# Cross attention and quantised FFN on one core: transposes of the activations moved from TensorE to DMA, with row-group bias matmuls, a deeper pipeline and another prologue

## The chip, the cores and the metric

The kernel runs on one core of one Trainium2 chip. The metric is device time in microseconds (us), the median of several executions; lower is better. The core has TensorE (PE in the rows; PEld is its weight load), VectorE (DVE), ScalarE (ACT), GpSimd (POOL), and SyncE (SP), which here only issues DMAs.

## The reference

x has 4 x 2048 rows of 512, the context 4 x 154 rows of 512. First cross attention with a mask `j % 2048 == i`: since the context has only 154 rows, query i < 154 sees only key i, and a query i >= 154 sees none, so its softmax is uniform over all 154. Queries and keys drop out: row i of the attention is `V[i] @ Wout + bout`, or the mean of V put through Wout. Then a feed-forward layer on 8-bit activations and ternary weights:

```
x = x + attention(context)
h = layernorm(layernorm(x)) * gamma + beta
xq, sx = round(h * 127 / max|h|), 127 / max|h|      # per row
h = gelu((xq @ w1q.T) / (sx * sw1) + b1)            # 512 -> 2048
hq, sh = round(h * 127 / max|h|), 127 / max|h|
x = x + (hq @ w2q.T) / (sh * sw2) + b2              # 2048 -> 512
```

w1q and w2q are `clip(round(w / mean|w|), -1, 1)`, made on the chip; sw1 and sw2 are the weight scales, `1 / mean|w|`.

## The kernel before, in words

The 8192 rows are 64 tiles of 128 rows (rotated by two tiles, so that the first need only the mean row of batch 0). Every engine has a program of its own, written out by hand in order; semaphores tie them. The main part is a loop of steps s = 0..66 in which each engine works on tiles at different distances.

Weights are in SBUF as bf16 (`w1q`, `w2q`). A matmul contracts over the 128 partitions, so both activations must be brought into the form [feature, row] first. TensorE does that with an identity matrix:
- `transpose_h` (L684 to L689) turns the rounded x tile, 4 blocks of 128x128, into PSUM `p_xT` (L688); ACT copies it out to `xqT` (`evac_x`, L416).
- L738 does the same with the rounded hidden tile `hround`, 16 blocks into `p_hT`; ACT copies them out in two halves to `hqT` (L452).

In step s TensorE does: the hidden transposes of tile s-2, layer one of tile s (L751, 16 matmuls into the four banks of `p_ffn1`), the x transposes of tile s+1, layer two of tile s-2 (L766, 16 matmuls into `p_y`). DVE adds the bias to layer one with the scale `xdeq` and takes it out of PSUM (L572, two halves), ACT applies the gelu in place (L438), DVE takes the maximum (L579) and makes the step and the scale (L582, L585), ACT rounds (L459). DVE then adds layer two's result to x (L654), SP stores it (L261). DVE's statistics and maximum (L544, L534) and POOL's additions of attention, gamma, beta and b2 (L290, L302, L304, L322), its rounding (L311) and small scale operations (L308, L315) feed the x side.

The prologue multiplies Wv and Wout first (`wvo`, L695, fp32), then the context rows with the product (L708 tail rows, L713 the four times 128 first rows), and makes the ternary weights (L500 to L504, L411). The mean row is spread over a tile by L718.

Of the kernel before, what the change touches and what calls it, by code (L numbers as in the profile page):

```python
# [6 lines left out]
I16 = mybir.dt.int16  # L40
ALU = mybir.AluOpType
# [3 lines left out]
P = 128  # L45
# [17 lines left out]
MAGIC = ROUND + OFFSET


def block_program(nc, x, ctxT, wvT, wout, bout, w1T, b1, w2T, b2, gamma, beta, out, tail_rows):
    es = ExitStack()
    with es:
# [6 lines left out]
        def sem(name):  # L75
# [33 lines left out]
        xdeq = sb("xdeq", [P, 8])  # L109
        hmax = sb("hmax", [P, 8])  # L110
# [22 lines left out]
        ones = sb("ones", [P, P])  # L133


        p_ffn1 = ps("p_ffn1", [P, HID])
        p_hT = ps("p_hT", [P, KH, P], BF16)
        p_xT = ps("p_xT", [P, KD, 2 * P], BF16)
        p_y = ps("p_y", [P, D])
        p_mean = p_xT[:, :, :].rearrange("p k n -> p (k n)").bitcast(FP32)  # L140
        p_wsum = p_hT[:, :, :].rearrange("p k n -> p (k n)").bitcast(FP32)


        ins_loaded = [sem(f"ins_loaded{i}") for i in range(KI)]
        ctx_loaded = sem("ctx_loaded")
        w1_loaded = [sem(f"w1_loaded{k}") for k in range(2)]
        w2_loaded = [sem(f"w2_loaded{k}") for k in range(4)]
        vec_loaded = sem("vec_loaded")
        b1_loaded = sem("b1_loaded")
        ones_set, ident_set = sem("ones_set"), sem("ident_set")  # L150
        wvo_done, wvo_copied = sem("wvo_done"), sem("wvo_copied")
        ctx_means, tail_gathered = sem("ctx_means"), sem("tail_gathered")
        attn_done, attn_copied = sem("attn_done"), sem("attn_copied")
        mean_done, mean_copied = sem("mean_done"), sem("mean_copied")
        pick_set = sem("pick_set")
        tail_stored = sem("tail_stored")
        attn_spread = [sem(f"attn_spread{b}") for b in range(B)]
        wparts_done = [sem(f"wparts_done{j}") for j in range(2)]
# [8 lines left out]
        x_loaded = [sem(f"x_loaded{r}") for r in range(8)]  # L167
# [3 lines left out]
        xstd_done, xgamma_done, xnormed = sem("xstd_done"), sem("xgamma_done"), sem("xnormed")  # L171
        xmax_done, xstep_done, xscale_ready = sem("xmax_done"), sem("xstep_done"), sem("xscale_ready")
        xdeq_ready, xround_done = sem("xdeq_ready"), sem("xround_done")
        xT_done, xqT_ready = sem("xT_done"), sem("xqT_ready")
        ffn1_done, bias_done, gelu_done = sem("ffn1_done"), sem("bias_done"), sem("gelu_done")
        hmax_done, hstep_done, hscale_ready = sem("hmax_done"), sem("hstep_done"), sem("hscale_ready")
        hdeq_ready, hround_done = sem("hdeq_ready"), sem("hround_done")
        hT_done, hqT_ready = sem("hT_done"), sem("hqT_ready")
        ffn2_done, y_ready = sem("ffn2_done"), sem("y_ready")
        y_stored = [sem(f"y_stored{r}") for r in range(4)]  # L180

        def col(t, c):

            return t[:, c % 8:c % 8 + 1]

        def live(i, c, ahead):

            return not isinstance(i, int) or 0 <= BODY * i + c + ahead < T

        def run(eng, step, first=0):  # L190


            for s in range(first, T + 3):
                step(s // BODY, s % BODY)

        def w_piece(j, n):

            return w1_raw[n // 2][:, n % 2, :] if j == 0 else w2_raw[:, n * HID:(n + 1) * HID]

        def wq_piece(j, n):  # L200

            return w1q[:, n, :] if j == 0 else w2q[:, 4 * n:4 * n + 4, :].rearrange("p k n -> p (k n)")

        block = es.enter_context(nc.Block())


        @block.sync
# [594 lines left out]
```

## Time and profile before

| | |
|---|---|
| median of 3 runs | 596.89 us (596.06 to 596.98) |
| profiled execution | 597.54 us |
| its span | 595.7 us |
| matmuls of layer one, tile 0, start | 61.31 us |
| matmuls of layer one, tile 3 | 87.93 to 91.33 us |
| one tile in the middle of the run | 8.03 us |
| granted TensorE clock, mean | 0.986 |

The span is from the first to the last instruction in the profile. A group's mean is the duration of one instruction; matmuls overlap, so the distance between two is shorter than the duration of one. "Idle before" is the time that the engine stood still ahead of the group, with what ended it behind the arrow.

### The profile page before, as it was taken

What the parts mean: (1) busy time and instruction counts of PE and PEld (TensorE: products, weight loads), DVE (VectorE), ACT (ScalarE), POOL (GpSimd) and SP (SyncE); (2) the same over time, 40 slices, a digit from 0 to 9 for tenths busy, and PEclk for the clock granted to TensorE, in tenths of its full rate; (3) what the DMA queues carried; (4) which work ended last, traced back from release to release, by engine and by line L of the source; (5) the groups of instructions that cost most, each with busy time, mean ns of one, the idle gap of its engine ahead of it and who ended that gap; (6) DMA issues with size and microseconds to landing.
All of it is one profiled execution on the core that took longest, in us unless ns stands there. A gap on an engine that the chain in (4) does not pass through costs nothing.

```text
span 595.7 us, 9691 instructions
## 1 busy us (share of the span) xinstructions
PE 568.9 (95%) x3374; PEld 295.4 (50%) x3438; DVE 513.4 (86%) x803; ACT 434.6 (73%) x412; POOL 449.9 (76%) x584
## 2 busy tenths in 40 slices
PE   6979777999999999999999999999999999999996
PEld 2434333555555555555555555555555555555553
DVE  0286998999999999999999999999999999998773
ACT  0046854787887788788778878877877787787784
POOL 0006879999898888889888988988888898887410
PEclk9979888999999999999999999999999999999999
DMA  8986512222221222222122222222222221300011
GB/s 317 411 278 244 173 30 60 72 72 71 72 53 57 71 73 70 72 72 54 55 70 73 72 70 72 48 62 71 70 73 72 72 49 58 89 36 19 37 36 54
DMA packets 26438, 53.24 MB, mean 89 GB/s; under 512 B 2729, under 2 KB 2729, under 8 KB 25749
## 3 DMA queue, kind: packets, MB, share of 16 engines
q1 hardware_dynamic: 24708, 49.25, 26.8%
q10 hardware_dynamic: 1680, 3.36, 1.6%
q8 instruction: 28, 0.46, 0.3%
q14 instruction: 22, 0.17, 0.1%
HBM read 35.60 MB, written 17.00 MB: 88 GB/s over the span
## 4 chain that ended last, share of the span: by engine, by line
PE 84%; DVE 7%; DMA 4%; issue 2%; POOL 1%; ACT 1%; ACTq 1%; POOLq 0%
PE p_y L766 36%; PE p_ffn L751 34%; PE p_hT L738 9%; DMA xb<-ctxT 4%; PE p_xT L688 2%; DVE hid L572 1%; DVE hmax L579 1%; PE p_y L708 1%; DVE wpart L509 1%; ACTq L400 1%; POOL x L290 1%; DVE hx L528 1%; DVE stat L544 1%; DVE w2q L504 1%; DVE xb L477 0%
## 5 line engine op out<-in xcount | busy, mean ns | idle before, releaser
L766 PE MATMUL p_y<-w2q,hqT 128*128 128x512 bf16 x1023 | 234.8, 383 | 7.0 <-DVE y L654 3.5
L751 PE MATMUL p_ffn<-w1q,xqT 128*128 128x512 bf16 x961 | 219.6, 381 | 6.9 <-ACT xqT L416 3.7
L459 ACT ACTIVATE hround<-hid,hscale 128x2048 f32<-128x2048 f32 x64 | 128.2, 2003 | 74.6 <-DVE hscale L585 74.6
L572 DVE SCALAR_TENSOR_TENSOR hid<-p_ffn,xdeq,b_b 128x1024 f32<-128x1024 f32 x128 | 163.4, 1279 | 0.6 <-issue 0.6
L766 PEld LDWEIGHTS p_y<-w2q,hqT 128*128 128x128 bf16 x1024 | 98.3, 99 | 116.1 <-issue 5.4
L751 PEld LDWEIGHTS p_ffn<-w1q,xqT 128*128 128x128 bf16 x1024 | 97.8, 98 | 111.3 <-ACT xqT L416 3.7
L579 DVE TENSOR_REDUCE hmax<-hid 128x1 f32<-128x2048 f32 x64 | 145.6, 2275 | 0.1
L438 ACT ACTIVATE hid<-hid 128x1024 f32<-128x1024 f32 x128 | 134.4, 1051 | 14.9 <-DVE hid L572 14.9
L452 ACT ACTIVATE hqT<-p_hT 128x1024 bf16<-128x1024 int16 x128 | 123.9, 1020 | 23.4 <-PE p_hT L738 23.4
L290 POOL TENSOR_TENSOR x<-x,attn 128x512 f32<-128x512 f32 x64 | 81.7, 1278 | 46.6 <-ACT attn L422 46.6
L304 POOL TENSOR_TENSOR hx<-hx,beta_b 128x512 f32<-128x512 f32 x63 | 80.6, 1279 | 4.9
L302 POOL TENSOR_TENSOR hx<-hx,gamma_b 128x512 f32<-128x512 f32 x63 | 81.0, 1286 | 1.8 <-DVE hx L528 1.8
L322 POOL TENSOR_TENSOR xb<-x,b_b 128x512 f32<-128x512 f32 x64 | 81.8, 1278 | 0.0
L654 DVE SCALAR_TENSOR_TENSOR y<-p_y,hdeq,xb 128x512 f32<-128x512 f32 x64 | 48.0, 750 | 37.3 <-PE p_y L766 37.2
L738 PEld LDWEIGHTS p_hT<-ident,hround 128*128 128x128 bf16 x1024 | 62.4, 98 | 16.4 <-ACT hround L459 2.0
L308 POOL TENSOR_TENSOR xdeq<-xstep,wmean 128x1 f32<-128x1 f32 x64 | 28.5, 446 | 53.6 <-DVE xscale L676 49.3
L738 PE MATMUL p_hT<-ident,hround 128*128 128x128 bf16 x1024 | 67.6, 219 | 1.1 <-ACT hround L459 1.1
L311 POOL TENSOR_SCALAR hx<-hx,xscale 128x512 f32<-128x512 f32 x64 | 44.9, 701 | 0.0
L544 DVE BATCH_NORM_STATS2 stat<-x 128x6 f32<-128x512 f32 x64 | 43.7, 683 | 1.2 <-POOL x L290 1.2
L534 DVE TENSOR_REDUCE xmax<-hx 128x1 f32<-128x512 f32 x64 | 43.3, 676 | 1.7 <-POOL hx L304 1.7
L296 POOL TENSOR_TENSOR rstd<-var_e,neg_half 128x1 f32<-128x1 f32 x64 | 35.8, 559 | 5.3
L416 ACT ACTIVATE xqT<-p_xT 128x512 bf16<-128x512 int16 x64 | 36.9, 576 | 0.8 <-PE p_xT L688 0.8
(58 smaller groups left out, 286.7 us busy)
## 6 DMA issues: line engine op xcount, KB each, us to landing
x<-x SPq DMA_DIRECT2D x64, 256.0 KB, 3.0
out<-y SPq DMA_DIRECT2D x64, 256.0 KB, 3.2
raw<-w2T SPq DMA_DIRECT2D x4, 1024.0 KB, 9.1
raw<-wout ACTq DMA_DIRECT2D x8, 256.0 KB, 7.7
raw<-wvT SPq DMA_DIRECT2D x8, 256.0 KB, 7.1
hid<-w1T SPq DMA_DIRECT2D x2, 1024.0 KB, 14.9
hround<-w1T SPq DMA_DIRECT2D x2, 1024.0 KB, 20.2
attn<-tail_rows SPq DMA_DIRECT2D x7, 256.0 KB
```

Of the source, the lines that this page charges most:

```text
L290: pool.tensor_tensor(x1[:, c, :], x1[:, c, :], a, ALU.add).then_inc(x1_ready, 1)
L302: pool.tensor_tensor(h, h, gamma_b[:, :], ALU.mult).then_inc(xgamma_done, 1)
L304: pool.tensor_tensor(h, h, beta_b[:, :], ALU.add).then_inc(xnormed, 1)
L322: pool.tensor_tensor(xb[:, c % 8, :], x1[:, c % 8, :], b2_b[:, :], ALU.add)\
L438: nc.scalar.activation(g, g, ACT.Gelu).then_inc(gelu_done, 1)
L452: nc.scalar.activation(hqT[:, c % 2, 8 * h:8 * h + 8, :], p_hT[:, 8 * h:8 * h + 8, :].bitcast(I16), ACT.Copy, bias=-float(OFFSET)).then_in ...
L459: nc.scalar.activation(hround[:, (c - 1) % 2, :], hid[:, (c - 1) % 2, :], ACT.Copy, scale=col(hscale, c - 1), bias=MAGIC).then_inc(hround_ ...
L572: nc.vector.scalar_tensor_tensor(hid[:, c % 2, h * HALF:(h + 1) * HALF], p_ffn1[:, h * HALF:(h + 1) * HALF], col(xdeq, c), b1_b[:, h * HAL ...
L579: nc.vector.tensor_reduce(col(hmax, c), hid[:, c % 2, :], AX.X, ALU.max, apply_absolute_value=True).then_inc(hmax_done, 1)
L738: tr = nc.tensor.transpose(p_hT[:, k, :], low[:, k * P:(k + 1) * P], ident[:, :])
L751: mm = nc.tensor.matmul(p_ffn1[:, n * D:(n + 1) * D], xqT[:, c % 2, k, :], w1q[:, k, n * D:(n + 1) * D], start=(k == 0), stop=(k == KD - 1))
L766: mm = nc.tensor.matmul(p_y[:, :], hqT[:, c % 2, k, :], w2q[:, k, :], start=(k == 0), stop=(k == KH - 1))
```

## The change

- **x transposed by DMA.** ACT rounds x to 16-bit integers (`xi`), POOL widens them to bf16 (`xq`), SP issues a transposing DMA of 128 x 640 elements of 2 bytes (`transpose_x`, L213) into `xqT`. The fifth block of 128 columns holds 1 / (scales) of the row, split in three bf16 parts.
- **Hidden tile transposed by DMA.** ACT rounds to 8-bit integers (`hq8`, L486); SP issues a transposing DMA over them as 16-bit words, two features to a word (`transpose_h`, L221), into `hT8`; DVE and ACT each widen one half to bf16 in `hqT` (L656, L493). The rows of `w2q` are laid out in pairs to fit.
- **Bias by matmul.** The four matmuls of L801 take the fifth block, 32 partitions for each bank, times `b1rows` (b1 in three bf16 parts), with `tile_position=(32 * g, 0)`; so the accumulated PSUM times `xdeq` contains b1, and ACT's gelu reads PSUM itself (L479). DVE's L572 is gone.
- **Layer two three tiles behind** (`LAG = 3`, was 2), `p_y` in two banks (`py`), x tiles in a ring of 16 in which the result is made in place.
- **x side:** gamma is applied by DVE together with the mean (L623), the factor 1/std by ACT (L464), statistics and scales for two tiles at a time, POOL's additions over two tiles at once.
- **Prologue:** V^T = Wv^T ctx^T is made first (L770 for the tail, L784 for the main rows), then times Wout (L749, and L760 in the first three steps of the main loop); weights are loaded in other pieces on both queues; b1 is split by POOL and stored by 12 small DMAs.

```diff
-                if live(i, c, -2):
-                    pe.wait_ge(hround_done, s - 1)
...
-                    for k in range(KH):
-                        tr = nc.tensor.transpose(p_hT[:, k, :], low[:, k * P:(k + 1) * P], ident[:, :])
...
-                if live(i, c, 1):
-                    pe.wait_ge(xqT_ready, s + 1)
-                    transpose_h(s + 1, c + 1)
...
+            for s in range(T + LAG):
+                if live(s):
+                    pe.wait_ge(xT_landed[s % 4], 16 * (s // 4 + 1))
...
+                        pe.wait_ge(gelu_done, 2 * s)
+                    xT = xqT[:, (s // 2) % 2, s % 2, :, :]
+                    for g in range(4):
+                        nc.tensor.matmul(p1[:, g * D:(g + 1) * D], xT[32 * g:32 * g + 32, KD, :],
+                                         b1rows[32 * g:32 * g + 32, :], start=True, stop=False,
+                                         tile_position=(32 * g, 0))
...
+                if s == 0:
+                    out_rows(1, pa[:, :])
+                elif s == 1:
+                    weight_total(1)
+                    out_rows(2, py[:, 0, :])
+                elif s == 2:
+                    out_rows(3, py[:, 1, :])
+                    pe.wait_ge(wmean_done[1], 1)
+                    out_rows(0, pb[:, :])
...
+                    pe.wait_ge(hcast_dve, t + 1)
+                    pe.wait_ge(hcast_act, t + 1)
```

```diff
+            def transpose_h(t):
+                sp.wait_ge(hround_done, t + 1)
+                if t >= 2:
+                    sp.wait_ge(hcast_dve, t - 1)
+                    sp.wait_ge(hcast_act, t - 1)
+                sp.dma_start_transpose(hT8[:, t % 2, :].bitcast(I16).rearrange("p (j n) -> p j n", j=NJ),
+                                       hq8[:, t % 2, :].bitcast(I16)).then_inc(hT_landed[t % 4], 16)
...
+            for s in range(T + LAG + 2):
+                if live(s - LAG - 1):
+                    t = s - LAG - 1
+                    sp.wait_ge(y_ready, t + 1)
+                    sp.dma_start(out[t * P:(t + 1) * P, :], xr[:, t % XS, :]).then_inc(y_stored[t % XS], 16)
+                if live(s - 1):
+                    transpose_h(s - 1)
...
+                if s >= 3 and live(s + 11):
+                    load_x(s + 11)
...
+                if s % 2 == 1:
+                    for t in (s + 3, s + 4):
+                        if live(t):
+                            transpose_x(t)
```

ACT and DVE in the main loop of the changed kernel:

```diff
+                if live(s - 1):
+                    round_h(s - 1)
+                if live(s):
+                    gelu(s, 0)
+                if live(s - 2):
+                    widen_h(s - 2)
+                if live(s):
+                    gelu(s, 1)
+                if s % 2 == 0:
+                    for t in (s + 4, s + 5):
+                        if live(t):
+                            times_std(t)
+                else:
+                    for t in (s + 3, s + 4):
+                        if live(t):
+                            round_x(t)
...
+                if live(s - 2):
+                    widen_h(s - 2)
+                if live(s - LAG - 1):
+                    result(s - LAG - 1)
+                if s % 2 == 0 and live(s + 4):
+                    for t in (s + 4, s + 5):
+                        statistics(t)
+                    for t in (s + 4, s + 5):
+                        centre(t)
+                if s % 2 == 1 and live(s + 3):
+                    x_scale(s + 3)
+                if live(s):
+                    hidden_scale(s)
```

On TensorE in the main loop there stood before (L738 hidden transposes, L751 layer one, L688 x transposes, L766 layer two):

```order
L766 MATMUL p_y<-w2q,hqT 128x512 x16
L738 MATMUL p_hT<-ident,hround 128x128 x16
L751 MATMUL p_ffn<-w1q,xqT 128x512 x16
L688 MATMUL p_xT<-ident,hx 128x128 x4
L766 MATMUL p_y<-w2q,hqT 128x512 x16
L738 MATMUL p_hT<-ident,hround 128x128 x16
```

and now (L801 bias, L808 layer one, L832 layer two):

```order
L801 MATMUL p<-b1rows,xqT 128x512 x4
L808 MATMUL p<-w1q,xqT 128x512 x16
L832 MATMUL py<-w2q,hqT 128x512 x16
L801 MATMUL p<-b1rows,xqT 128x512 x4
L808 MATMUL p<-w1q,xqT 128x512 x16
L832 MATMUL py<-w2q,hqT 128x512 x16
```

Both groups of transposes are gone, and one group of four bias matmuls has come in ahead of layer one.

On TensorE between the prologue and the first tiles there now stands (L784 V^T of the main rows, L755 the sum over partitions of the weights' absolute values, L760 attention rows of one batch):

```order
L784 MATMUL p<-hqT,hid 128x512 x28
L755 MATMUL pb<-wsum,hT 128x1
L784 MATMUL p<-hqT,hid 128x512 x4
L801 MATMUL p<-b1rows,xqT 128x512 x4
L808 MATMUL p<-w1q,xqT 128x512 x16
L760 MATMUL pa<-wout,vTm_own 128x512 x5
L760 MATMUL pa<-wout,attn 128x512 x3
L801 MATMUL p<-b1rows,xqT 128x512 x4
L808 MATMUL p<-w1q,xqT 128x512 x16
L755 MATMUL pb<-wsum,hT 128x1
L760 MATMUL py<-wout,vTm_own 128x512 x5
L760 MATMUL py<-wout,attn 128x512 x3
```

The total of the first weights' sizes now stands behind 28 matmuls of V^T, and the attention rows have moved from ahead of layer one to between its first tiles.

On SP in the main loop there stood before, per tile, a load (L258) and a store (L261):

```order
L258 DMA x<-x 128x512
L261 DMA out<-y 128x512
L258 DMA x<-x 128x512
L261 DMA out<-y 128x512
L258 DMA x<-x 128x512
```

and now (L264 store, L221 hidden transpose, L187 load, L213 x transposes, for two tiles at once):

```order
L213 DMA_TRANSPOSE xqT<-xq 128x5x128 x2
L264 DMA out<-xr 128x512
L221 DMA_TRANSPOSE hT<-hq 128x8x128
L187 DMA xr<-x 128x512
L264 DMA out<-xr 128x512
L221 DMA_TRANSPOSE hT<-hq 128x8x128
L187 DMA xr<-x 128x512
L213 DMA_TRANSPOSE xqT<-xq 128x5x128 x2
L264 DMA out<-xr 128x512
```

SP's queue has taken up two transposes a tile, and each hidden transpose stands behind a store.

## Rows read from the trace of the kernel before

**Rows 1.** Page, part 1: busy us (share of the span) and instructions per engine.
```profile
PE 568.9 (95%) x3374; PEld 295.4 (50%) x3438; DVE 513.4 (86%) x803; ACT 434.6 (73%) x412; POOL 449.9 (76%) x584
```

**Rows 2.** Page, part 4: shares of the span in the chain of waits, by line.
```profile
PE p_y L766 36%; PE p_ffn L751 34%; PE p_hT L738 9%; DMA xb<-ctxT 4%; PE p_xT L688 2%; DVE hid L572 1%; DVE hmax L579 1%; PE p_y L708 1%; DVE wpart L509 1%; ACTq L400 1%; POOL x L290 1%; DVE hx L528 1%; DVE stat L544 1%; DVE w2q L504 1%; DVE xb L477 0%
```

**Rows 3.** Timeline of PE, one tile: start us, us, engine, line, operation.
```profile
305.12 0.39 PE L688 MATMUL p_xT<-ident,hx 128*128 128x128 bf16 x4
...
305.35 3.62 PE L766 MATMUL p_y<-w2q,hqT 128*128 128x512 bf16 x16
...
308.80 1.06 PE L738 MATMUL p_hT<-ident,hround 128*128 128x128 bf16 x16
...
309.91 3.40 PE L751 MATMUL p_ffn<-w1q,xqT 128*128 128x512 bf16 x15
...
313.15 0.39 PE L688 MATMUL p_xT<-ident,hx 128*128 128x128 bf16 x4
```

**Rows 4.** Timeline of PE in the prologue.
```profile
5.14 30.38 PE L695 MATMUL p_ffn<-raw 128*128 128x512 f32 x64 [5.14 <-DMA raw<-wvT]
...
61.31 3.40 PE L751 MATMUL p_ffn<-w1q,xqT 128*128 128x512 bf16 x15
...
87.93 3.40 PE L751 MATMUL p_ffn<-w1q,xqT 128*128 128x512 bf16 x15 [0.65 <-ACT xqT L416]
```

**Rows 5.** Timeline of the end: PE and DVE.
```profile
577.92 3.62 PE L766 MATMUL p_y<-w2q,hqT 128*128 128x512 bf16 x16
...
592.47 0.75 DVE L654 SCALAR_TENSOR_TENSOR y<-p_y,hdeq,xb 128x512 f32<-128x512 f32 x1 [4.88 <-PE p_y L766]
```

**Rows 6.** Groups of instructions from 200 to 500 us: busy us, mean ns | idle before.
```profile
L751 PE MATMUL p_ffn<-w1q,xqT 128*128 128x512 bf16 x560 | 127.1, 379 | 1.9
...
L579 DVE TENSOR_REDUCE hmax<-hid 128x1 f32<-128x2048 f32 x37 | 84.2, 2276 | 0.0
L438 ACT ACTIVATE hid<-hid 128x1024 f32<-128x1024 f32 x75 | 78.9, 1052 | 9.1 <-DVE hid L572 9.1
L459 ACT ACTIVATE hround<-hid,hscale 128x2048 f32<-128x2048 f32 x38 | 76.1, 2002 | 37.2 <-DVE hscale L585 37.2
L452 ACT ACTIVATE hqT<-p_hT 128x1024 bf16<-128x1024 int16 x74 | 71.7, 1020 | 13.6 <-PE p_hT L738 13.6
...
L322 POOL TENSOR_TENSOR xb<-x,b_b 128x512 f32<-128x512 f32 x38 | 48.2, 1269 | 0.0
...
L654 DVE SCALAR_TENSOR_TENSOR y<-p_y,hdeq,xb 128x512 f32<-128x512 f32 x37 | 27.8, 751 | 16.1 <-PE p_y L766 16.0
L544 DVE BATCH_NORM_STATS2 stat<-x 128x6 f32<-128x512 f32 x38 | 26.0, 683 | 0.0
...
L311 POOL TENSOR_SCALAR hx<-hx,xscale 128x512 f32<-128x512 f32 x37 | 25.6, 693 | 0.0
...
L528 DVE TENSOR_SCALAR hx<-x,mv,rstd 128x512 f32<-128x512 f32 x37 | 19.1, 516 | 0.0
L308 POOL TENSOR_TENSOR xdeq<-xstep,wmean 128x1 f32<-128x1 f32 x37 | 17.8, 480 | 27.5 <-DVE xscale L676 27.5
...
L585 DVE RECIPROCAL hscale<-hstep 128x1 f32<-128x1 f32 x38 | 6.2, 164 | 1.3
```

**Rows 7.** DMA issues with KB and median us to landing, and one issue in the timeline.
```profile
x<-x SPq DMA_DIRECT2D x64, 256.0 KB, 3.0
out<-y SPq DMA_DIRECT2D x64, 256.0 KB, 3.2
...
305.19 0.43 SPq L261 DMA_DIRECT2D out<-y  x1
```

**Rows 8.** Stretches: length, busy us per engine, granted clock, DMA share, GB/s.
```profile
core 0: us, PE busy (x) PEld busy (x) DVE busy (x) ACT busy (x) POOL busy (x), PEclk, DMA share, GB/s
290.00:380.00 90.00, 89.42 (x571) 47.52 (x581) 84.40 (x136) 72.45 (x69) 78.65 (x100) 1.00 0.25 70
```

More of the change, by code:

```diff
@@ L159, in block_program @@
+        wabs_act = [sem(f"wabs_act{j}") for j in range(2)]
         wsum_done = [sem(f"wsum_done{j}") for j in range(2)]
@@ L186, in live @@
[L186 to L202, printed above, removed]
+        xdeq_ready, rr_done, rrows_ready = sem("xdeq_ready"), sem("rr_done"), sem("rrows_ready")
@@ new lines, in _ @@
+            abs_w2(5, 4)
+            abs_w2(1, 5)
+            times_std(2)
+            times_std(3)
+            abs_w2(3, 6)
+            abs_w2(7, 7)
+            round_h(0)
+            round_x(2)
+            round_x(3)
+            gelu(1, 0)
+            gelu(1, 1)
+            for j in (5, 1, 3, 7):
+                round_weights(1, j)
+            times_std(4)
+            times_std(5)
+            round_h(1)
+            round_x(4)
+            round_x(5)
+            gelu(2, 0)
+            widen_h(0)
@@ new lines, in attn_rows @@
+            def attn_rows(b, bank, n):
+                dve.wait_ge(attn_done, n)
+                nc.vector.tensor_tensor(attn[:, 3 * b, :], bank, bout_b[:, :], ALU.add).then_inc(attn_copied, 1)
+            abs_w1(0, 0)
+            statistics(0)
+            abs_w1(2, 1)
+            statistics(1)
+            dve.wait_ge(gamma_loaded, 16)
+            centre(0)
+            abs_w1(4, 2)
+            centre(1)
+            abs_w1(6, 3)
+            x_scale(0)
+            mean(0)
+            round_weights(0, 0)
@@ L679, in _ @@
-            run(dve, step, 3)
+            for t in (2, 3):
+                statistics(t)
+            dve.wait_ge(tail_stored, 16)
+            centre(2)
+            centre(3)
+            abs_w2(4, 0)
+            abs_w2(6, 1)
+            hidden_scale(0)
+            x_scale(2)
+            abs_w2(0, 2)
+            abs_w2(2, 3)
+            attn_rows(1, pa[:, :], 1)
+            mean(1)
+            for n, (d, a) in enumerate(((4, 5), (6, 1), (0, 3), (2, 7))):
+                round_weights(1, d)
+                dve.wait_ge(wround_dve[1], n + 1)
+                clip(1, d)
+                dve.wait_ge(wround_act[1], n + 1)
+                clip(1, a)
@@ new lines, in weight_total, with out_rows @@
+            def weight_total(j):
+                pe.wait_ge(wsum_done[j], 1)
+                nc.tensor.matmul(pb[:, j:j + 1], ones[:, :], wsum[:, j:j + 1], start=True, stop=True)\
+                    .then_inc(wtotal_done[j], 1)
+            def out_rows(b, bank):
+                for m in range(KI):
+                    mm = nc.tensor.matmul(bank, vTm[m][:, b * P:(b + 1) * P], wout[:, m, :],
+                                          start=(m == 0), stop=(m == KI - 1))
+                mm.then_inc(attn_done, 1)
@@ L768, in step @@
                     mm.then_inc(ffn2_done, 1)
-            run(pe, step)
 def kernel(x, ctx_1024, L0_xattn_Wq, L0_xattn_Wkv, L0_xattn_Wout, L0_xattn_bout,
```

1011 lines of the change are left out of this document (506 added, 505 removed).

## The prediction

> **What bounds the kernel now.** I read the busy shares first: TensorE (PE) is busy 95% of the span, VectorE (DVE) 86%, GpSimd (POOL) 76%, ScalarE (ACT) 73% [rows 1]. A share alone does not name the bound, so the chain of waits came next: 36% of the span is the second layer's matmuls (L766), 34% the first layer's (L751), 9% the 16 transposes of the hidden tile (L738) and 2% the 4 transposes of the input tile (L688) [rows 2]. The timeline of one tile shows why: each group on TensorE starts where the one before ends, and L688 comes again after 313.15 - 305.12 = 8.03 us [rows 3]. Inside it L766 takes 308.80 - 305.35 = 3.45 us for 16 matmuls (0.216 each), and L688 305.35 - 305.12 = 0.23 us. From 308.80 to 313.15 are 4.35 us for L738 and L751; less 3.45 for L751, which has the same shape, L738 costs 0.90 us (the row shows 15 of its 16 matmuls). The steady state is bound by TensorE and by nothing else: 6.90 us of matmuls and 1.13 us of transposes in a tile.
>
> The run has three pieces. The prologue: the first matmuls of layer one start at 61.31, those of tile 3 run from 87.93 to 91.33 [rows 4]. Then 60 tiles at TensorE's pace up to the start of L766 for tile 61 at 577.92, right behind the last matmul of layer one. Then a tail up to the span's end at 595.7: 17.8 us, of which the last DVE operation starts at 592.47 [rows 5]. So 91.3 + 60 x 8.11 + 17.8 = 595.7. The profiled execution took 597.54, 1.84 more than its span, and stands 0.65 above the median of 596.89.
>
> **The change in the steady state, TensorE.** All 20 transposes go: -1.13 us a tile. Four bias matmuls come in ahead of layer one, each on 32 rows of the array, 512 columns, each into its own bank. The trace has none of this kind. From below: beside one another they cost one slot, 0.22. From above: one after another 4 x 0.216 = 0.86, and twice the array's run-out where the shape changes; a matmul of L751 shows 379 ns where its neighbours are 216 apart [rows 3, 6], so a run-out is 0.16 and the top is 0.86 + 0.33 = 1.19. I take one slot and one run-out, 0.38. TensorE then needs 6.90 + 0.38 = 7.28 us a tile (7.12 to 8.09). The Trainium skill, TensorEngine Tiling (Array Packing), Key Properties, says that tiles work in parallel but that changing the tiling mode drains the engine; by that two drains a tile, 7.44. No row here shows it either way.
>
> **The other engines at 7.28.** ACT, per tile: one rounding of 2048 (2.00), two gelus of 1024 (1.05 each, now straight from PSUM with a scale), half of the widening (1.02), and two operations of 512 for x (0.58 each by 1.05 for 1024 with the fixed part kept): 6.3 us. DVE loses two 1.28 us bias additions and gets the other half of the widening; nearest rows are L528 (512 in 0.52, so 1.0) and L579 (2048 in 2.28, so 1.14): I take 1.0. In an even step it has widening 1.0, result 0.75, two statistics with their small operation 1.7, two centrings 1.4 (like L654), two half maxima 2.4, two small ones 0.33: 7.6. In an odd step widening 1.0, result 0.75, x scale of two tiles 1.2 + 0.33, maxima and small ones 2.7: 6.0. POOL, per two tiles: six times 512 elements at 1.27, two widenings of 0.69, nine small ones of at most 0.48: 13.3, so 6.7 a tile [rows 6]. All lie under 7.28, but DVE and ACT hang on each other: hscale lets ACT round (2.04), then gelu, widening, gelu (to 5.05), then DVE's second half maximum and two small ones (to 6.6). An odd step can't be shorter than that 6.6, an even one not than 7.6: 7.1 on average, 0.2 under TensorE. The cover is thin.
>
> **The transposes by DMA.** They leave TensorE for SP's queue: per tile one of 256 KB (hidden, in byte pairs) and one of 160 KB (x). The trace has no transposing DMA. The nearest rows are plain copies of 256 KB, 3.0 us from issue to landing for a load and 3.2 for a store, and 0.43 us of SP's queue for an issue [rows 7]. I take 3.2 for L, issue to landing, as the lower end, and twice that, 6.4, as the upper. What waits: SP sends the store of result t-4 before the transpose of tile t-1; that store waits for DVE's result, which stands in DVE's order behind the widening of tile t-2, which waits for the landing of transpose t-2. So a tile can't be faster than L + widening 1.0 + result 0.75 + issue 0.43 = L + 2.2. With 3.2 that is 5.4, hidden; it decides from L = 5.1 on, and behind it SP's x transposes and loads would be late too. Second layer three tiles behind instead of two costs nothing on TensorE, and gives the landing a whole tile.
>
> **The prologue.** Before, an fp32 matmul of 512 columns takes 0.86 us at full clock (64 records, two to a matmul, in 30.38 us from 5.14, with a slow start) [rows 4]. New work: 32 fp32 matmuls of 108 columns, between 0.18 (by columns) and 0.86, I take 0.4: 12.8; 8 tail rows of 512: 6.9; 32 for V, of which 28 lie ahead of the weight mean: 24; 32 for the attention rows: 27.5. Before there were 32 + 4 + 1 + 16, about 46 us; now about 76. Context sums at about 10 (5 to 20), + 12.8 + 6.9 + 3 for tail row and mean + 24 = 57; + 4 for mean, scale and POOL's small operations, + 3.2 for the first transpose and some widening: layer one starts at about 65, 4 later than the 61.3. From there TensorE has three tiles of layer one, 3 x 3.8 = 11.5, and the 27.5 of attention rows: 104. But DVE takes attention row 3 in order, at 97; behind it stand statistics and centring (3.1), the hidden scale of tile 1 (2.8), the x scale (1.6); then ACT's x rounding (1.5) and the gelus of tile 2 with a widening (3.1): 109.8. Layer one of tile 3 can only follow: it ends at about 114 (108 by TensorE alone, 125 if the slower ends add up). That is 23 us later than 91.3.
>
> **The sum.** Prologue 114 + 60 x 7.28 = 437 + tail. The tail before was 17.8; in it 1.28 of bias, 0.9 of transposes, and one evacuation of 0.9 go, a transpose of 3.2 comes: 17.9. Span 568.7, with 1.84 outside 570.5; less the 0.65 by which the profiled run stands over the median, 570. Per tile -0.83 against 8.11, 50 us; prologue +23.
>
> **Rivals.**
> Transposes late: if a transposing DMA takes twice the plain copy, L = 6.4, the period is 6.4 + 2.2 = 8.6, and the time 114 + 516 + 17.9 + 3.2 + 1.2 = 652. Break-even with 596.9 is a period of (596.9 - 1.2 - 131.9) / 60 = 7.73, so L = 5.5. For it: every tile gives SP four issues instead of two, and the loop goes through three engines; against it: the DMA engines are busy only 0.25 of the steady state [rows 8] and a copy has 1.9 us in hand. The Trainium skill has both: VectorE: DVE Perf Modes, The three transpose paths, gives 1309 ns for one 128x128 block by DMA, eight of them one after another 10.5 us, which would be an estimate of 12.7 a tile and some 900 us; DMA: Bandwidth & Descriptors, Latency and other measured facts, gives 350 to 400 GB/s in the contiguous case, and then L stays near the copy's. No run here shows it.
> Bias matmuls one after another with both run-outs: 8.09 a tile, 114 + 485 + 17.9 + 1.2 = 618, slower. It decides from 0.83 for the four.
> DVE and ACT as the bound: POOL and DVE disturb each other or a hop costs more; 0.2 more at three hops of the loop gives 7.6 to 7.7 and 590 to 596. The 0.2 us of slack speaks for it.
> A lighter prologue (108) with bias at one slot: 108 + 427 + 19.1 = 554.
>
> **How the numbers follow.** Forecast (period 7.12 to 7.45, prologue 108 to 120; 554 to 586) 0.52; DVE and ACT bind (586 to 598) 0.15; transposes late 0.21; bias in series 0.10; quicker than 554 0.02. Forecast and quicker are faster, 0.54, of the second case 0.13: 0.67. Within 0.2% (some 1.2 us, about what a measurement here can tell from no change): 0.02 of the second case and 0.01 of the late transposes, 0.03. Slower: 0.20 + 0.10 = 0.30. The range goes from 548 to 640, which leaves out the late transposes' far half. The likeliest case's own range is 554 to 586.
>
> **What would show it.** Right: L832 comes again on TensorE every 7.2 to 7.5 us with less than 0.1 idle; L801's four records start nearly together; hidden transposes land 3 to 4 us after issue; DVE's L656 has no idle before it; layer one of tile 3 ends at 108 to 120. Wrong: idle before L656 or L493 ended by the DMA (late transposes); L801 starts 0.216 apart; idle before L801 released by the gelu L479 (DVE and ACT bind); ffn1 of tile 3 after 125.

## The result, and the profile after

| | before | after |
|---|---|---|
| median | 596.89 us (595.99 to 597.60, 5 runs) | 601.40 us (600.60 to 602.29, 5 runs) |
| ratio to before, 95% interval | | 1.0079 (1.0062 to 1.0095) |
| span of the profiled execution | 595.7 us | 600.0 us |
| layer one of tile 3 ends | 91.3 us | 124.8 us |
| the next 60 tiles, each | 8.11 us | 7.63 us |
| from the end of the last layer one to the end of the span | 17.8 us | 17.3 us |

The changed kernel is 0.8% slower, where 570 us was forecast. The three pieces add up: the prologue is 33.5 us later, 60 tiles bring back 28.7 (0.48 each), the tail 0.5, together +4.3 = 600.0 - 595.7. The forecast had +23 and -50.

The busy shares and the chain of waits of the changed kernel, from its page, answer to [rows 1, 2]:

```profile
PE 545.9 (91%) x2471; PEld 240.5 (40%) x2518; DVE 458.5 (76%) x724; ACT 423.7 (71%) x417; POOL 378.5 (63%) x435
...
DVE 36%; POOL 27%; PE 18%; issue 11%; DMA 3%; ACT 2%; SPq 1%; POOLq 0%; ACTq 0%; DVEq 0%
POOL hx L339 13%; POOL xr L343 7%; DVE xmax L629 6%; DVE hmax L644 6%; DVE xstep L632 6%; DVE hid L640 6%; DVE stat L615 6%; PE py L832 5%; PE p L808 4%; PE p L784 4%; DVE xr L665 3%; POOL var_e L328 3%; POOL rstd L331 2%; PE py L760 2%; DM
```

TensorE is still the busiest, with 91%, but only 18% of the chain is its own. VectorE and GpSimd, at 76% and 63%, carry 63% of it. One line stands out: `xstep L632`, an instruction over two numbers per partition, has as large a share as a reduction over 1024.

TensorE's timeline over one pair of tiles (start, length, engine, line), where [rows 3] had a group of transposes ahead of each layer:

```profile
296.69 0.39 PE L801 MATMUL p<-b1rows,xqT 32*128 32x512 bf16 x4
297.02 3.63 PE L808 MATMUL p<-w1q,xqT 128*128 128x512 bf16 x16
300.48 3.62 PE L832 MATMUL py<-w2q,hqT 128*128 128x512 bf16 x15
304.64 0.40 PE L801 MATMUL p<-b1rows,xqT 32*128 32x512 bf16 x4 [0.54 <-ACT hid L479]
304.97 3.63 PE L808 MATMUL p<-w1q,xqT 128*128 128x512 bf16 x16
308.43 3.62 PE L832 MATMUL py<-w2q,hqT 128*128 128x512 bf16 x16
311.98 0.39 PE L801 MATMUL p<-b1rows,xqT 32*128 32x512 bf16 x4
```

The pair takes 311.98 - 296.69 = 15.29 us, 7.65 a tile. The four bias matmuls take 0.33 (304.64 to 304.97), layer one 3.46, layer two 3.55 up to the bias matmuls behind it (308.43 to 311.98; 3.45 in [rows 3]): 7.34 us of work. Once in the pair TensorE then waits for ScalarE's gelu, here 0.54 us.

The wait is made elsewhere. VectorE in the same pair, from one result (L665) on:

```profile
300.03 0.74 DVE L665 SCALAR_TENSOR_TENSOR xr<-py,hdeq,xr 128x512 f32<-128x512 f32 x1
...
302.20 0.18 DVE L617 BATCH_NORM_AGGREGATE mv<-stat 128x2 f32<-128x6 f32 x1
302.30 1.40 DVE L623 SCALAR_TENSOR_TENSOR hx<-xr,mv,gamma_b 128x512 f32<-128x512 f32 x2
...
306.39 0.77 DVE L656 CAST hqT<-hT 128x1024 bf16<-128x1024 int8 x1
307.08 0.74 DVE L665 SCALAR_TENSOR_TENSOR xr<-py,hdeq,xr 128x512 f32<-128x512 f32 x1
309.42 1.22 DVE L629 TENSOR_REDUCE xmax<-hx 128x2 f32<-128x1024 f32 x1 [1.60 <-POOL hx L339]
310.67 1.20 DVE L632 TENSOR_SCALAR xstep<-xmax 128x2 f32<-128x2 f32 x1
311.91 0.17 DVE L635 RECIPROCAL xscale<-xstep 128x2 f32<-128x2 f32 x1
```

and GpSimd:

```profile
302.48 0.61 POOL L328 TENSOR_SCALAR var_e<-mv 128x2 f32<-128x2 f32 x1 [3.03 <-DVE mv L617]
303.24 1.04 POOL L331 TENSOR_TENSOR rstd<-var_e,neg_half 128x2 f32<-128x2 f32 x1
304.25 2.36 POOL L343 TENSOR_TENSOR xr<-xr,b_b 128x1024 f32<-128x1024 f32 x1
306.57 2.81 POOL L339 TENSOR_TENSOR hx<-hx,beta_b 128x1024 f32<-128x1024 f32 x1
309.35 0.19 POOL L374 TENSOR_TENSOR hdeq<-hstep,wmean 128x1 f32<-128x1 f32 x1
309.49 2.36 POOL L324 TENSOR_TENSOR xr<-xr,attn 128x1024 f32<-128x1024 f32 x1
```

Read together they are a ring, once round in 15.3 us: VectorE's statistics (to 302.38) release GpSimd's L328; GpSimd goes through the deviation, the b2 addition L343 and the beta addition L339 (to 309.38); only that releases VectorE's maximum L629, after 1.60 us in which VectorE, in order, stands still; then come L632, the hidden maxima, the result, and the statistics of the next pair. L632 starts at 310.67 and ends at 311.87, 0.02 after GpSimd's L324 (309.49 + 2.36 = 311.85). L339 takes 2.81 instead of 2.36 where VectorE's cast L656 (306.39 to 307.16) started ahead of it and still runs.

The prologue on TensorE answers to [rows 4]:

```profile
66.30 0.61 PE L801 MATMUL p<-b1rows,xqT 32*128 32x512 bf16 x4 [4.85 <-DMA xqT<-xq]
...
96.40 4.45 PE L760 MATMUL py<-wout,vTm_own 128*128 128x512 f32 x10
100.69 2.74 PE L760 MATMUL py<-wout,attn 128*128 128x512 f32 x6
...
119.27 0.62 PE L801 MATMUL p<-b1rows,xqT 32*128 32x512 bf16 x4 [8.98 <-ACT hid L479]
120.22 4.73 PE L808 MATMUL p<-w1q,xqT 128*128 128x512 bf16 x15 [0.33 <-issue]
```

and the one row of VectorE on which it hangs:

```profile
103.47 0.69 DVE L670 TENSOR_TENSOR attn<-py,bout_b 128x512 f32<-128x512 f32 x1 [9.93 <-PE py L760]
```

Layer one starts at 66.3 (65 was forecast). VectorE then stands still for 9.93 us in `attn_rows(3)`, whose matmuls TensorE does last but one, with the statistics of tiles 4 and 5 and the hidden scale of tile 1 behind it; TensorE in turn stands still for 8.98 us. Behind that the granted clock is 0.50 from 119.2 to 121.0, the lower of the two levels, and 1.00 from 125 on; layer one of tile 3 takes 4.57 up to the start of layer two, instead of 3.46. The same happens behind the gap of 4.85 us ahead of tile 0: the granted clock is 0.58 from 66.3 to 72.7.

The transposing DMAs, median us to landing, answer to [rows 7]:

```profile
xqT<-xq SPq DMA_TRANSPOSE x64, 2.6
hT<-hq SPq DMA_TRANSPOSE x64, 3.1
```

3.1 for the hidden tile: neither late nor a bound. From 200 to 500 us no wait of any engine is put down to a transpose.

### The profile page after: what moved, and what is told of

The parts are those of the page before. It is cut to its first block, busy times and chain, and to the rows that moved or that the text cites. A ratio compares the mean times of both kernels' runs of the same rounds, so it can differ in the third digit from the quotient of the medians.

```text
span 600.0 us, 7964 instructions
## 1 busy us (share of the span) xinstructions
PE 545.9 (91%) x2471; PEld 240.5 (40%) x2518; DVE 458.5 (76%) x724; ACT 423.7 (71%) x417; POOL 378.5 (63%) x435
## 4 chain that ended last, share of the span: by engine, by line
DVE 36%; POOL 27%; PE 18%; issue 11%; DMA 3%; ACT 2%; SPq 1%; POOLq 0%; ACTq 0%; DVEq 0%
POOL hx L339 13%; POOL xr L343 7%; DVE xmax L629 6%; DVE hmax L644 6%; DVE xstep L632 6%; DVE hid L640 6%; DVE stat L615 6%; PE py L832 5%; PE p L808 4%; PE p L784 4%; DVE xr L665 3%; POOL var_e L328 3%; POOL rstd L331 2%; PE py L760 2%; DMA hid<-wv_d 2%
## 5 line engine op out<-in xcount | busy, mean ns | idle before, releaser
L808 PE MATMUL p<-w1q,xqT 128*128 128x512 bf16 x995 | 232.4, 384 | 2.9 <-issue 1.9
L832 PE MATMUL py<-w2q,hqT 128*128 128x512 bf16 x1006 | 230.0, 379 | 0.9
L486 ACT ACTIVATE hq<-hid,hscale 128x2048 int8<-128x2048 f32 x64 | 128.2, 2004 | 71.4 <-DVE hscale L650 71.4
L832 PEld LDWEIGHTS py<-w2q,hqT 128*128 128x128 bf16 x1024 | 100.2, 98 | 120.8
L808 PEld LDWEIGHTS p<-w1q,xqT 128*128 128x128 bf16 x1024 | 96.0, 99 | 123.5 <-issue 20.1
L479 ACT ACTIVATE hid<-p,xdeq 128x1024 f32<-128x1024 f32 x128 | 140.5, 1099 | 0.4 <-PE p L808 0.4
L339 POOL TENSOR_TENSOR hx<-hx,beta_b 128x1024 f32<-128x1024 f32 (+1 forms) x33 | 87.8, 2662 | 11.9 <-ACT hx L464 11.9
L324 POOL TENSOR_TENSOR xr<-xr,attn 128x1024 f32<-128x1024 f32 (+1 forms) x33 | 76.5, 2319 | 28.6 <-ACT attn L498 24.8
L328 POOL TENSOR_SCALAR var_e<-mv 128x2 f32<-128x2 f32 x32 | 19.5, 609 | 104.0 <-DVE mv L617 103.8
L640 DVE TENSOR_REDUCE hid<-hid 128x1 f32<-128x1024 f32 x64 | 77.3, 1207 | 8.0 <-ACT hid L479 8.0
L629 DVE TENSOR_REDUCE xmax<-hx 128x2 f32<-128x1024 f32 x32 | 39.0, 1219 | 57.4 <-POOL hx L339 57.4
L644 DVE TENSOR_REDUCE hmax<-hid 128x1 f32<-128x1025 f32 x64 | 78.1, 1221 | 5.3 <-ACT hid L479 3.2
L343 POOL TENSOR_TENSOR xr<-xr,b_b 128x1024 f32<-128x1024 f32 x32 | 75.4, 2355 | 0.0
L493 ACT ACTIVATE hqT<-hT 128x1024 bf16<-128x1024 int8 x64 | 66.9, 1046 | 2.4 <-DMA hT<-hq 2.4
L464 ACT ACTIVATE hx<-hx,rstd 128x512 f32<-128x512 f32 x64 | 42.6, 716 | 19.6 <-POOL rstd L331 19.6
L656 DVE CAST hqT<-hT 128x1024 bf16<-128x1024 int8 x64 | 49.0, 765 | 7.9 <-DMA hT<-hq 7.1
L801 PE MATMUL p<-b1rows,xqT 32*128 32x512 bf16 x256 | 25.8, 390 | 29.4 <-ACT hid L479 24.4
L665 DVE SCALAR_TENSOR_TENSOR xr<-py,hdeq,xr 128x512 f32<-128x512 f32 x64 | 47.5, 742 | 3.3 <-PE py L832 3.3
L623 DVE SCALAR_TENSOR_TENSOR hx<-xr,mv,gamma_b 128x512 f32<-128x512 f32 x64 | 45.2, 746 | 0.0
```

The source lines that it names most:

```text
L324: pool.tensor_tensor(xtile(t, n), xtile(t, n), a, ALU.add).then_inc(x1_ready, n)
L339: pool.tensor_tensor(htile(t, n), htile(t, n), bb, ALU.add).then_inc(xnormed, n)
L343: pool.tensor_tensor(xtile(t, 2), xtile(t, 2), b2_b[:, :, :].broadcast_to([P, 2, D]), ALU.add)\
L479: nc.scalar.activation(hid[:, t % 2, h * HALF:(h + 1) * HALF], p1[:, h * HALF:(h + 1) * HALF], ACT.Gelu, scale=col(xdeq, t)).then_inc(gelu ...
L486: nc.scalar.activation(hq8[:, t % 2, :], hid[:, t % 2, 0:HID], ACT.Copy, scale=col(hscale, t))\
L493: nc.scalar.activation(hqT[:, t % 2, NJ // 2:, :, :], hT8[:, t % 2, HALF:].rearrange("p (j t e) -> p j e t", e=2, t=P), ACT.Copy).then_inc ...
```

## The experiments

Each kernel is timed against the kernel before on the same chip. Period is the mean over the 60 tiles from the end of tile 3's layer one to the end of the last (for kernel 8 that of a pair in the middle). Where an edit adds or takes out lines, the line numbers behind it shift.

| kernel | median us | ratio (95%) | span | tile 3 done | period |
|---|---|---|---|---|---|
| changed kernel | 601.4 | 1.0079 (1.0062 to 1.0095) | 600.0 | 124.8 | 7.63 |
| 1 step in two columns apart | 584.7 | 0.9789 (0.9753 to 0.9826) | 582.9 | 124.3 | 7.35 |
| 2 beta ahead of b2 | 599.6 | 1.0040 (1.0022 to 1.0057) | 598.2 | 123.6 | 7.62 |
| 3 both of these | 606.4 | 1.0156 (1.0119 to 1.0193) | 603.5 | 122.8 | 7.72 |
| 4 attention rows 3 later on DVE | 590.7 | 0.9894 (0.9860 to 0.9929) | 588.8 | 113.2 | 7.64 |
| 5 edits 1 and 4 | 575.1 | 0.9638 (0.9590 to 0.9687) | 573.4 | 114.4 | 7.36 |
| 6 as 5, no bias matmuls | 572.6 | 0.9582 (0.9553 to 0.9612) | 568.7 | 110.6 | 7.34 |
| 7 step over three columns | 603.6 | 1.0103 (1.0063 to 1.0144) | 599.2 | 123.5 | 7.64 |
| 8 as 5, layer two two tiles behind | 619.4 | 1.0363 (1.0333 to 1.0394) | 618.4 | | 8.0 |
| 9 as 5, rows 1 in the gap | 577.2 | 0.9670 (0.9647 to 0.9693) | 574.4 | 115.9 | 7.35 |
| 10 as 6, no b2 addition | 562.5 | 0.9433 (0.9407 to 0.9459) | 559.1 | 110.4 | 7.18 |
| 11 short attention addition | 583.9 | 0.9782 (0.9760 to 0.9804) | 581.3 | 123.6 | 7.34 |

**1. The step instruction in two.**

```diff
-                nc.vector.tensor_scalar(col(xstep, t, 2), col(xmax, t, 2), EPS, 1.0 / QMAX,
-                                        ALU.max, ALU.mult).then_inc(xstep_done, 1)
-                dve.wait_ge(xstep_done, u + 1)
+                for i in range(2):
+                    nc.vector.tensor_scalar(col(xstep, t + i), col(xmax, t + i), EPS, 1.0 / QMAX,
+                                            ALU.max, ALU.mult).then_inc(xstep_done, 1)
+                dve.wait_ge(xstep_done, 2 * u + 2)
```

> DVE's x step (L632, one instruction over two columns, 1.20 us while POOL adds attention) is issued as two single-column instructions. Theory A, a ring through DVE and POOL sets the pace (statistics, POOL's 1/std, b2, beta, DVE's x maximum, step, hidden maxima, and again), and the two-column step waits in it for POOL's running addition: the step takes about 0.15 twice, the pair of tiles loses 0.85 to 0.9 of its 15.32 us, 30 pairs give some 26 us, about 575 us. Rival B, the wait passes on to the reciprocal behind it, which has two columns too: no gain, 601. Rival C, TensorE waits for the gelu for a reason of its own: no gain.

Measured: 584.7, 17 us less in span, for one more instruction. VectorE's rows of one pair of this kernel, and GpSimd's beside them:

```profile
302.40 0.21 DVE L633 TENSOR_SCALAR xstep<-xmax 128x1 f32<-128x1 f32 x2
302.65 0.17 DVE L636 RECIPROCAL xscale<-xstep 128x2 f32<-128x2 f32 x1
```

```profile
301.22 2.37 POOL L324 TENSOR_TENSOR xr<-xr,attn 128x1024 f32<-128x1024 f32 x1
```

Both columns together take 0.21 us in the middle of GpSimd's L324 (301.22 to 303.59). The reciprocal over two columns lies there too and takes 0.17; it was never slow. The chain of waits of the steady part is now TensorE alone:

```profile
by line: PE p L809 53.9%; PE py L833 43.2%; PE p L802 4.1%
```

The gain stops there. The step lost 0.99 of the ring's 15.3 us, which by itself would give 7.16 a tile (kernel 6 will show the ring at 7.28), but TensorE needs 7.34. So the gain that I expected, 26 us, was too large, because it went past TensorE's bound; the mechanism holds.

**2 and 3. The beta addition ahead of the b2 addition on GpSimd**, alone and with edit 1.

```diff
-                        add_b2(s + 4)
                         add_beta(s + 4, 2)
+                        add_b2(s + 4)
```

> POOL adds beta ahead of b2 instead of behind it, so that DVE's x maximum no longer waits for the addition of b2 (2.36 us). Theory A: beta starts when ACT's times-std is done, 0.8 us earlier, and ends 1.0 earlier; the two-column step then waits for the addition of b2 instead of that of attention. The pair loses about 0.9 us, about 575 us. Rival B: POOL's later work (widening of x, 1.1 us later) takes the place, no gain. Rival C: no gain.

> Both edits, the split step and beta ahead of b2. Theory A: the ring falls to some 13.5 us a pair and TensorE is the bound at 3.46 + 3.45 + 0.33 = 7.24 a tile: 600 less 30 x 0.84 = 575 us, hardly less than either alone. If the two gains add (550), TensorE's floor is lower than read from its rows. Rival C: no gain.

Measured: 599.6 alone, within 2 us of the changed kernel, and 606.4 with edit 1, which is 22 us worse than edit 1 alone. The gain of theory A is there in kernel 2 (L632 has a mean of 0.46 us instead of 1.20), but something takes its place, as rival B said: from 200 to 500 us VectorE's cast waits 30.2 us in all for the hidden transpose in kernel 2 and 26.6 in kernel 3, and not at all in the changed kernel. The swap releases VectorE's maximum sooner and GpSimd's later work later. The chain of waits of kernel 3 shows who needs that later work:

```profile
299.67 1.00 POOL xq L370
...
300.69 1.20 SPq L213
...
302.00 1.22 SPq L213
...
303.27 0.57 SPq L264
...
303.94 3.14 DMA hT<-hq
```

GpSimd's widening of x (L370) ends later, SP's two x transposes (L213) wait for it and hold the queue 1.2 us each, and the hidden transpose stands behind them. This is read from the chain; no edit tried it alone. VectorE then waits for the transpose, and runs into GpSimd; its timeline, and GpSimd's:

```profile
307.11 2.73 DVE L657 CAST hqT<-hT 128x1024 bf16<-128x1024 int8 x1 [1.88 <-DMA hT<-hq]
```

```profile
304.62 2.35 POOL L339 TENSOR_TENSOR hx<-hx,beta_b 128x1024 f32<-128x1024 f32 x1 [1.58 <-ACT hx L464]
306.93 2.36 POOL L343 TENSOR_TENSOR xr<-xr,b_b 128x1024 f32<-128x1024 f32 x1
```

The cast takes 2.73 us here and 0.69 when GpSimd is idle (at 299.43 in the changed kernel); GpSimd's L343 ends at 309.29, and the cast 0.55 later.

**4. The prologue: attention rows 3 behind tile 4's scale on VectorE.**

```diff
             attn_rows(2, py[:, 0, :], 2)
-            attn_rows(3, py[:, 1, :], 3)
...
             x_scale(4)
+            attn_rows(3, py[:, 1, :], 3)
             widen_h(0)
```

> In the prologue DVE takes attention row 3 behind the statistics, centring, hidden scale of tile 1 and x scale of tiles 4 and 5, not ahead of them. Theory P: DVE stood 9.9 us for this row (93.5 to 103.5), with the gelu of tile 2 and so layer one of tile 3 behind it; TensorE stood 9.0 us before layer one of tile 3. That idle time goes nearly whole, and with it the lowered granted clock after it: 590 us, layer one of tile 3 from about 111 instead of 120. Rival: POOL's additions or ACT are late in its place, gain under 3 us.

Measured: 590.7. TensorE has no gap from 84.5 on; layer one of tile 3 ends at 113.2, 11.6 us sooner, and the period stays at 7.64:

```profile
109.45 0.39 PE L801 MATMUL p<-b1rows,xqT 32*128 32x512 bf16 x4
109.78 3.63 PE L808 MATMUL p<-w1q,xqT 128*128 128x512 bf16 x16
```

**5. Both edits that helped.** Its diff is that of 1 and of 4.

> The two edits that helped, together: the quantization step of a pair as two one-column instructions, and the addition of attention rows 3 on VectorE behind tile 4's scale. Theory A (the two losses are independent, one in the steady loop, one in the prologue, each paid once): 600.0 - 17.1 - 11.2 = a span of about 572, time 573, layer one's tile 3 at 109.5 to 113.2, a tile every 7.34 us with TensorE always busy. Rival B (the steady loop had been catching up part of the late prologue, so that one gain eats the other): 580 or more.

Measured: 575.1, 3.6% under the kernel before and 4.4% under the changed one. The two losses are independent: spans 600.0 - 17.1 - 11.2 = 571.7 against 573.4.

**6. Without the bias matmuls**, on kernel 5.

```diff
-                    for g in range(4):
-                        nc.tensor.matmul(p1[:, g * D:(g + 1) * D], xT[32 * g:32 * g + 32, KD, :],
...
-                                                  start=False, stop=(k == KD - 1))
+                                                  start=(k == 0), stop=(k == KD - 1))
```

> As the run with both edits, and the four bias matmuls of each tile left out (b1 is not added; the first product of each column block starts the accumulation instead). Theory A (TensorE's instruction stream is now the bound and the bias costs it 0.33 us of a tile): 64 x 0.33 = 21 us less where nothing else binds; the ring of VectorE and ScalarE, which I put at 7.0 to 7.2 of a tile, takes some of it back, so a tile every 7.05 to 7.2 and a time of 552 to 564. Rival B (the ring of VectorE, ScalarE and GpSimd binds at the same 7.3): no change, 573.

Measured: 572.6, only 2.4 less. Of the 4.7 us between the spans, 3.8 are tile 3, done earlier, and the period falls by 0.02. The ring stands right behind TensorE. Its links in the chain of waits of this kernel:

```profile
300.51 1.45 POOL xr L343
...
302.83 2.82 POOL hx L339
...
305.67 1.23 DVE xmax L629
```

L343 starts again at 315.08, 14.57 us later: 7.28 a tile. So the bias matmuls cost next to nothing as the program stands. On TensorE itself they take 0.43 and not only 0.33: here layer two lasts 3.45 up to layer one, and with the bias matmuls between them 3.55 up to these.

**10. Without the b2 addition too**, and without VectorE's wait for it, from tile 4 on.

```diff
-                        add_b2(s + 4)
                         add_beta(s + 4, 2)
```

> As the run without the bias matmuls, with GpSimd's addition of b2 left out too from tile 4 on (neither b1 nor b2 is added). Without the bias matmuls the tile stayed at 7.28, on a ring through GpSimd in which the b2 addition stands ahead of the beta addition. Theory A (that addition is a link of the ring): GpSimd's addition of beta can start 1.4 us earlier in each pair, TensorE becomes the bound at 7.01 a tile, and the time falls by up to 60 x 0.27 = 16 us, to 557 to 560. Rival B (the ring waits for ScalarE's scaling by the deviation, or for VectorE's order, and b2 only filled the wait): no more than 4 us, 569 to 573.

Measured: 562.5, 10 less than kernel 6: L343 is a link of the ring. Of its 2.36 us only about 0.85 came free, because GpSimd's beta addition now waits 1.51 us for ScalarE (L463). At 7.18 the period is still above TensorE's 6.90 (with neither bias matmuls nor the switch ahead of them). The chain then runs almost wholly through VectorE, 14.29 us a pair in the middle, and VectorE is busy 98% from 200 to 500 us. But part of that is waiting for GpSimd:

```profile
311.68 2.30 DVE L656 CAST hqT<-hT 128x1024 bf16<-128x1024 int8 x1
```

GpSimd's beta addition runs from 311.08 to 313.43, and the cast ends at 313.98. The mean of the cast is 1.55 us here against 0.69 alone, 1.7 us more a pair; without it VectorE's work would be about 12.6 a pair (an estimate), under TensorE's.

**7. The step over three columns**, a test of what makes the instruction slow. `trio` lays out the columns of a pair four apart, and the third holds a constant.

```diff
-                nc.vector.tensor_scalar(col(xstep, t, 2), col(xmax, t, 2), EPS, 1.0 / QMAX,
+                nc.vector.tensor_scalar(trio(xstep, t, 3), trio(xmax, t, 3), EPS, 1.0 / QMAX,
```

> The changed kernel with the quantization step of a pair as one instruction over three columns (the third holds a constant that nobody uses), where it was two. Theory A (VectorE takes the instruction on two columns in a mode that pairs elements and needs the port it shares with GpSimd; an odd count keeps it out of that mode): the instruction takes 0.15 us beside GpSimd's work and the time falls as with two one-column instructions, to 585. Rival B (any instruction of this kind on more than one column waits for GpSimd): it stays at 1.2 us and the time at 601.

```profile
L640 DVE TENSOR_SCALAR xstep<-xmax 128x3 f32<-128x3 f32 x20 | 23.4, 1168 | 0.7
```

Measured: 603.6, and 1.17 us for the instruction. My theory that an odd count escapes fell; with one column it escapes, with two and with three it doesn't.

**11. GpSimd's attention addition made short**, with L632 as it was. From tile 8 on the attention is added to the first column only.

```diff
-                pool.tensor_tensor(xtile(t, n), xtile(t, n), a, ALU.add).then_inc(x1_ready, n)
+                w = 1 if t >= 8 else D
+                pool.tensor_tensor(xtile(t, n)[:, :, 0:w], xtile(t, n)[:, :, 0:w], a[:, :, 0:w], ALU.add)\
+                    .then_inc(x1_ready, n)
```

> The changed kernel, its two-column step instruction left as it is, with GpSimd's attention addition cut from 2 x 512 columns to 2 x 1 from tile 8 on (the attention is then added to the first column only). That addition (2.36 us) is what GpSimd is in the middle of when the step instruction comes. Theory A (the step instruction waits for GpSimd's running instruction): it takes 0.15 to 0.2 us in place of 1.20, the ring loses 1.03 us of a pair, and TensorE becomes the bound at 7.34 a tile: 584 to 586. Rival B (1.2 us is what the two-column form costs beside busy queues, whatever GpSimd runs): it stays at 1.2, and the time within 3 us of 601.

The step instruction in this kernel, from 200 to 500 us:

```profile
L634 DVE TENSOR_SCALAR xstep<-xmax 128x2 f32<-128x2 f32 x20 | 3.4, 169 | 0.7
```

Measured: 583.9. The same instruction in the same place takes 0.17 us once GpSimd is not in the middle of L324. The period falls to 7.34, TensorE's, as in kernel 1. The two kernels show the cause from both sides: the wait is for GpSimd's running instruction.

The Trainium skill, SBUF — State Buffer, SBUF: two separate sides, has the rule that one pair of SBUF ports is shared by VectorE and GpSimd as an exclusive lock, held for a whole instruction, and that a VectorE instruction needs it in its two-port modes, or with two SBUF inputs against a GpSimd instruction that reads SBUF. The Trainium skill, VectorE: DVE Perf Modes, What auto-detection actually checks, adds that a two-port mode with one source, source and destination in SBUF, is taken where their outermost non-unit dimensions are both even or equal. The traces agree: three columns in and three out (equal) waited 1.17 us, and two waited 1.20. One column has no such dimension, and it did not wait (0.15). Why the reciprocal over two columns did not wait either, no run here shows.

**8. Layer two only two tiles behind**, on kernel 5 (`LAG = 2`).

> As the run with both edits, with the second layer two tiles behind the first instead of three. From the end of layer one of a tile to the start of its layer two TensorE then has 4 x 3.5 = 14 us of other work; GELU 1.1, the maxima 2.5, rounding 2.0, the transposing DMA 3.1 and the widening 1.0 make 9.7 in series, plus the waits in the in-order streams. Theory A (the transposes have room enough without the third tile): within 3 us of the run with both edits, 570 to 576. Rival B (VectorE's and ScalarE's order puts the widening behind the next tile's work, so layer two waits in each tile): 0.3 to 0.6 us of a tile, 592 to 611.

Measured: 619.4, 8.0 us a tile, worse than either theory. The transposes have room; the third tile buys something else. TensorE and ScalarE in the middle of this kernel:

```profile
300.51 3.63 PE L809 MATMUL p<-w1q,xqT 128*128 128x512 bf16 x15
304.66 3.61 PE L833 MATMUL py<-w2q,hqT 128*128 128x512 bf16 x16 [0.53 <-issue]
```

```profile
302.50 1.11 ACT L479 ACTIVATE hid<-p,xdeq 128x1024 f32<-128x1024 f32 x1 [1.22 <-PE p L809]
303.52 1.05 ACT L493 ACTIVATE hqT<-hT 128x1024 bf16<-128x1024 int8 x1
```

This is rival B's mechanism, a little above its size. ScalarE's order is gelu of tile s, first half, then its half of the widening of tile s-2 (L493). The gelu waits for half of layer one of tile s, the widening stands behind it and ends at 304.57, and layer two of tile s-2 starts at 304.66; one tile on, L493 ends at 312.54 and L833 starts at 312.63. So in each tile layer two waits about 0.5 us for a widening that its own tile's transpose had long allowed (VectorE starts its half of the same tile at 307.19). With three tiles of distance layer two needs the widening of the step before. The profile puts this wait down to no releaser; the order of the program and the two pairs of times name it, and no edit tried it. VectorE's cast gets dearer too (a mean of 1.97 us, where kernel 5 has 1.02 and the changed kernel 0.73), but the cast for the tile of 312.63 ends at 309.83 and is not what layer two waits for.

**9. Attention rows 1 in TensorE's gap ahead of tile 0**, on kernel 5.

> As the run with both edits, with attention rows 1 (16 fp32 matmuls, 7.2 us) in TensorE's gap of 4.84 us ahead of the first bias matmuls instead of behind layer one of tile 0. Theory A (in the prologue TensorE is the bound from 67 on): 4.8 us less, and the clock doesn't fall; span 573.4 - 5 = 568.6, time 570. Rival B (VectorE's rounding of the second layer's weights and the pipeline's fill are as late as TensorE, and layer one of tile 0 now starts 3.4 later): 575 to 578.

Measured: 577.2 (span 574.4), no gain. Layer one of tile 0 is no longer slowed by the low clock (3.63 us instead of 5.80), but TensorE then waits 6.35 us for VectorE's sum of the second layer's weights, and tile 3 is done at 115.9 instead of 114.4:

```profile
85.50 0.59 PE L756 MATMUL pb<-wsum,hT 128*128 128x1 f32 x2 [6.35 <-DVE wsum L597]
```

## Why the prediction was wrong, point by point

The span is 31.3 us over the forecast's 568.7: 10.8 from the prologue (124.8 instead of 114), 21.1 from 60 periods (7.63 instead of 7.28), less 0.6 in the tail.

- **TensorE per tile, 7.28: nearly right.** 7.34 where TensorE is the bound. The four bias matmuls took 0.33 and the switch ahead of them 0.10, 0.43 against 0.38; the rival of matmuls in series (0.83 and more) is refuted. By my estimate of two drains, from the Trainium skill, TensorEngine Tiling (Array Packing), Key Properties, it would have been 7.44; the trace lies between.
- **The transposes, L = 3.2: right.** 3.1 and 2.6 to landing. The 10.5 us estimated from the 1309 ns of the Trainium skill, VectorE: DVE Perf Modes, The three transpose paths, is far from the trace: the page gives one block, and taking eight of them one after another was my step. Only SP's time was mis-sized: 1.2 us of its queue for a transpose against the 0.43 of a plain issue. No wait shows it in the changed kernel; in the chain of kernel 3 it stands ahead of the late transpose.
- **The step that failed: "All lie under 7.28, but DVE and ACT hang on each other".** I priced GpSimd by its sum (6.7 a tile; it is busy 63% of the span) and set it aside. But the x side goes VectorE, GpSimd, VectorE within each pair, in two in-order streams, and GpSimd was put in pairs of tiles: its stretch from the statistics to the maximum is 302.48 to 309.38, 6.9 us, during which VectorE runs out of other work. The loop that I did draw, VectorE with ScalarE at 7.1, was never seen to bind. Kernel 10, where b2 and the bias are gone, comes near it in number (7.15 in the middle), but by luck: its chain is VectorE alone, with 1.7 us a pair of a cast that waits for GpSimd.
- **Inside that step, one term: "x scale of two tiles 1.2 + 0.33".** The 0.33 turned out as 1.20 + 0.17. [Rows 6] have the small instructions of VectorE with one column only; the change gave them two. Its 1.03 us a pair kept the ring at 7.65, above TensorE's 7.34, and cost 17 us of the 50 forecast.
- **The rival "DVE and ACT as the bound", 7.6 to 7.7, had the right period and the sign on TensorE's idle row** (released by the gelu). It named in passing that POOL and DVE disturb each other, but as 0.2 us at three hops of the loop with ScalarE; what came was 1.03 us at one instruction of the ring with GpSimd. Its 590 to 596 missed through the prologue.
- **Prologue 114: 11 too early.** Layer one starts at 66.3 as forecast. I had VectorE take attention row 3 at 97; TensorE had it done only at 103.4 (layer one 1.3 later, the low clock in tile 0, a wait of 1.7 for the weights' sum), and what stands behind it on VectorE took 15.1 us instead of 12.1, then layer one at the low clock. Kernel 4 takes this term away, and tile 3 is done at 113.2.
- **Tail 17.9: right,** 17.3.

Kernel 5 is the forecast's sum with sizes off by little: tile 3 at 114.4 (114), a period of 7.36 (7.28), a tail of 17.3 (17.9), a span of 573.4 (568.7). That 114.4 meets 114 is partly chance: the 114 was summed along attention row 3 on VectorE, a path that kernel 5 no longer has, and by TensorE alone I had 108. The gain was there; two waits on VectorE hid it.

## What to carry to other kernels

When TensorE is relieved, draw the ring of the other engines for one whole period with every engine that a value passes through, GpSimd too, and not their sums; its length, not a busy share, is the next bound. When an instruction's shape changes, even from one column to two, price it anew and look at what GpSimd does at that moment. In an in-order stream, put the evacuation of a late result behind all that doesn't need it.

## What the runs showed of the hardware that was not expected

- A VectorE tensor-scalar instruction over two or three fp32 columns waits for GpSimd's running addition (1.20 and 1.17 us; over two columns 0.17 where that addition is short); over one column it doesn't (0.15), nor does a reciprocal over two (0.17).
- The same holds the other way: GpSimd's 2.36 us addition takes 2.81 when VectorE's int8 cast has started 0.18 us ahead of it, and the cast takes 0.69 alone and up to 2.73 beside GpSimd.
- Four matmuls of 32 rows and 512 columns, each in its own row group and bank, take 0.33 us together ahead of full-array ones.
- A transposing DMA from SBUF to SBUF lands its 256 KB in 3.1 us, and takes 1.2 us of SP's queue.
